# Row maxima as a stream of searches in two stages, paired float32r scores, and two score units ahead of the values

## The reference, cut to what matters

```
xn = layernorm(x)
q, k, v = split(xn @ w_qkv)          # 16 heads of 16
s = softmax(causal(q k^T / 4)) v @ w_out
f = xn
for i in range(6):
    f = gelu(f @ W1[i]^T + B1[i]) @ W2[i]^T + B2[i] + f     # 256 -> 1024 -> 256
    if i < 5: f = layernorm(f) * LN_G[i] + LN_B[i]
out = x + s * silu(f)
```

## Time and profile before

| what | us |
|---|---|
| runs of the kernel | 1800.85, 1801.35, 1807.49 (median 1801.35) |
| span of the profiled execution | 1806.1 |
| PE busy | 1716.2 |
| DVE busy | 1149.1 |
| ACT busy | 958.0 |
| POOL busy | 323.2 |

### The profile page before, as it was taken

One profiled execution on the slowest core, in us unless ns is written; L12 is line 12 of the kernel. 1 busy time (PEld: TensorE's weight loads), 2 busy tenths in 40 slices (PEclk: granted clock), 3 DMA queues, 4 the chain that ended last, 5 costly groups with the idle time before them and its releaser, 6 DMA issues. The chain is left out here.

```text
span 1806.1 us, 33624 instructions
## 1 busy us (share of the span) xinstructions
PE 1716.2 (95%) x11664; PEld 1312.9 (73%) x11664; DVE 1149.1 (64%) x2325; ACT 958.0 (53%) x1364; POOL 323.2 (18%) x317
## 2 busy tenths in 40 slices
PE   6979999999999999999999999997999989999947
PEld 5869999999999989999999998875444433444236
DVE  7846666666666656666666643366877866877326
ACT  5834555555555545555555554432666665666723
POOL 3511111111111111111111111110121211121214
PEclk9989999999999999999999999998999998999969
DMA  6940000000000000000000050003474754574113
GB/s 206 306 140 13 12 17 16 13 12 17 13 9 12 17 16 12 13 17 12 16 12 12 0 83 24 23 24 64 76 112 75 109 84 73 88 107 73 48 57 137
DMA packets 104427, 97.97 MB, mean 54 GB/s; under 512 B 26636, under 2 KB 88588, under 8 KB 104316
## 3 DMA queue, kind: packets, MB, share of 16 engines
q1 hardware_dynamic: 104256, 96.39, 23.9%
q10 hardware_dynamic: 60, 0.10, 0.0%
HBM read 62.15 MB, written 29.62 MB: 51 GB/s over the span
## 5 line engine op out<-in xcount | busy, mean ns | idle before, releaser
L626 ACT ACTIVATE m_hid<-m_h_ps,m_b1s 128x512 f32<-128x512 f32 x384 | 264.3, 688 | 571.0 <-PE m_h_ps L752 558.9
L687 DVE TENSOR_TENSOR m_hidl<-m_hid,m_hidh 128x512 fp32r<-128x512 f32 x384 | 307.4, 809 | 323.9 <-ACT m_hidh L628 322.8
L129 DVE TENSOR_REDUCE mx<-a_s_ps 128x1 f32<-128x512 f32 (+3 forms) x570 | 341.2, 656 | 91.3 <-PE a_s_ps L117 87.8
L1003 ACT ACTIVATE a_prob<-a_st_ps 128x1024 f32<-128x1024 f32 (+1 forms) x320 | 289.9, 938 | 168.5 <-PE a_st_ps L1153 123.0
L752 PE MATMUL m_h_ps<-xth,shared 128*128 (+1 forms) x768 | 269.8, 397 | 12.3 <-DVE shared L655 12.2
L763 PE MATMUL m_y_ps<-shared,m_hidh 128*128 128x256 f32 x1536 | 277.9, 281 | 0.0
L628 ACT ACTIVATE m_hidh<-m_h_ps,m_b1s 128x512 fp32r<-128x512 f32 x384 | 261.8, 682 | 0.0
L763 PEld LDWEIGHTS m_y_ps<-shared,m_hidh 128*128 128x128 f32 x1536 | 246.6, 189 | 12.0 <-DVE m_hidl L687 0.4
L602 POOL TENSOR_TENSOR y<-y,m_b2s 128x1024 f32<-128x1024 f32 x47 | 112.8, 2400 | 708.3 <-DVE y L663 708.3
L763 PE MATMUL m_y_ps<-m_w2h,m_hidh 128*128 128x256 f32 x768 | 217.9, 284 | 0.6 <-DVE m_hidl L687 0.3
L763 PE MATMUL m_y_ps<-shared,m_hidl 128*128 128x256 f32 x768 | 215.8, 281 | 0.0
(11 more groups left out here) (115 smaller groups left out, 2648.3 us busy)
## 6 DMA issues: line engine op xcount, KB each, us to landing
q_parts<-p_part SPq DMA_DIRECT2D x16, 384.0 KB, 3.5
k_parts<-p_part SPq DMA_DIRECT2D x16, 384.0 KB, 3.0
m_raw<-w1t SPq DMA_DIRECT2D x48, 128.0 KB, 2.2
m_raw<-w2t SPq DMA_DIRECT2D x48, 128.0 KB, 2.4
shared<-q_parts SPq DMA_DIRECT2D x48, 128.0 KB, 4.6
shared<-k_parts SPq DMA_DIRECT2D x48, 128.0 KB, 7.7
a_qs<-q_parts SPq DMA_DIRECT2D x48, 128.0 KB, 4.6
a_ks<-k_parts SPq DMA_DIRECT2D x48, 128.0 KB, 7.4
```

The lines of the kernel that those rows point to most:

```text
L129: return nc.vector.reduce_max(mx[:, half, first:first + heads, qt], scores, AX_X)
L626: nc.scalar.activation(hid[k % 2][:], h_ps[k % 2][:], ACT.Gelu, bias=b1s[s.par][:, k:k + 1])
L687: nc.vector.tensor_tensor(hidl[k % 4][:], hid[k % 2][:], hidh[k % 4][:].bitcast(F32), ALU.subtract).then_inc(low_done, 1)
L1003: nc.scalar.activation(prob[step % BUFS][:, j:j + heads, 0:hi - lo], unit_ps(unit), ACT.Exp).then_inc(exp_done, 1)
```

## The change

It touches nearly all of the file. In short:

* q and k are split into two float32r parts of float32 size. A stack has three parts, 48 rows a head, and two rows for the maximum. Two heads lie side by side, at partitions 0 and 64, and a product of scores is a pair of float32r matmuls, one on each half of the array's rows, into two banks. `max_pieces` gives 20 pieces a group.
* The class `MaxSearch` makes one sequence of 336 visits: for each group 20 pieces, and one turn of the maxima, placed after the fifth piece of the next group. A visit is a product on PE and a maximum on DVE. There are two PSUM banks for it, one a side. The mask at a diagonal is no product any more: DVE adds a mask tile and takes the maximum in one instruction (`tensor_tensor_reduce`). The first 209 visits are made in `mlp`, 9 in two slots, the rest in `attend`, spread over the first 14 groups. Search and scores have their own loads of the stacks; the maxima go through device memory.
* `mlp` is written out without loops. It holds the transposed rows of two groups only and turns each slot's rows in the slot before (47 turns in the loop and one ahead of it), works in `xres` in place, has one y buffer in PSUM (its sum in two halves), does one scaled pass on ACT and two on POOL, and no longer stores its rows.
* `project` loads and splits block 0's weights, and no longer stores turned rows.
* `attend` is written out, without a planner. Steps are 10 a group: the last key tile but two and the last of a half are one step of 384 + 128 columns. Each step's units are both issued, then the visits due, then the values of two steps before. `o_ps` has two buffers; DVE copies the output.
* `combine` reads the gate from `xres`.

The core of the diff:

```diff
-PARTS = 3
-STACK = 6 * HD
+PARTS = 2
+STACK = 3 * HD
 ROWS = STACK + PARTS
+SIDE = P // 2
+PAIR = 2
+N_GROUPS = BATCH * HG
+AHEAD = 10
...
+    def pe_visit(s, pe, s_ps, v):
+        m, p = s.visits[v]
+        if p == NP:
+            pe.wait_ge(s.nm_ready, m + 1)
+            pe.wait_ge(s.maxed, 2 * v)
+            s.nc.tensor.transpose(s_ps[0:PARTS * HG * QT, 0, 0:P], s.nm[:].rearrange("p a m -> p (a m)"), s.ident[:]).then_inc(s.done, 1)
+            return
...
+        for c in range(columns):
+            for side in range(2):
+                if c == 0 and v:
+                    pe.wait_ge(s.maxed, 2 * v - 1 + side)
+                rows = slice(SIDE * side, SIDE * side + STACK)
+                i = s.nc.tensor.matmul(s_ps[:, side, c * keys:(c + 1) * keys], s.q[m % 2][rows, first + c, qt * P:(qt + 1) * P],
+                                       s.k[m % 2][rows, first + c, half * BANK:half * BANK + keys], start=True, stop=True)
+        i.then_inc(s.done, 1)
...
+        if qt // HG != half:
+            s.nc.vector.reduce_max(mx[:, half, first::PAIR, qt], s_ps[:, :, 0:keys], AX_X).then_inc(s.maxed, 2)
+        else:
+            for side in range(2):
+                for c in range(columns):
+                    h = PAIR * side + first + c
+                    i = s.nc.vector.tensor_tensor_reduce(s.unused[:, v % 2, side, c * keys:(c + 1) * keys], s_ps[:, side, c * keys:(c + 1) * keys],
+                                                         s.causal[:, BANK - keys:BANK], 1.0, NEG, ALU.add, ALU.max, mx[:, half, h:h + 1, qt])
+                i.then_inc(s.maxed, 1)
...  (mlp)
+        VISITS = search.at[AHEAD, 0]
+        for v in range(VISITS):
+            slot, place = divmod(2 * v, 9)
+            AT.setdefault(CH * (1 + slot) + (1, 4, 4, 5, 5, 6, 6, 7, 7)[place], []).append(v)
...
+            for n in range(CHUNKS + 2):
+                if n < CHUNKS:
+                    up(n)
+                if n % CH == 2 and n // CH + 1 < SLOTS:
+                    turn(n // CH + 1)
+                if n >= 2:
+                    down(n - 2)
+                for v in AT.get(n, ()):
+                    search.pe_visit(pe, s_ps, v)
...  (attend)
+                if U >= 2:
+                    pe.wait_ge(exp_done, U - 1)
+                col = 0
+                for kt, lo, hi in STEPS[step][1]:
+                    for c in range(columns):
+                        for side in range(2):
+                            rows = slice(SIDE * side, SIDE * side + ROWS)
+                            to = st_ps[unit % 2][:, side, col + c * WIDTH[step]:col + c * WIDTH[step] + hi - lo]
+                            i = nc.tensor.matmul(to, ks[n % 2][rows, first + c, kt * P:(kt + 1) * P],
+                                                 qs[n % 2][rows, first + c, lo:hi], start=True, stop=True)
+                    col += hi - lo
+                i.then_inc(st_done, 1)
...
+            for at in range(ALL + LATE + 1):
+                n, step = divmod(at, NS)
+                if at < ALL:
+                    scores(n, FIRST_OF[step])
+                if at < ALL and LAST_OF[step] > FIRST_OF[step]:
+                    scores(n, LAST_OF[step])
+                for v in AT.get(at, ()):
+                    search.pe_visit(pe, s_ps, v)
+                if 0 <= at - LATE < ALL:
+                    values(at - LATE)
```

More of the change, by code:

```diff
@@ L102, in shared_stacks @@
[L102 to L118, removed]
@@ L121, in by_head @@
-def by_head(bank, piece):
-    _, _, _, heads, keys = piece
-    return bank[:, 0:heads * keys].rearrange("p (h n) -> p h n", n=keys)
-def row_max(nc, mx, scores, piece):
-    qt, half, first, heads, _ = piece
-    return nc.vector.reduce_max(mx[:, half, first:first + heads, qt], scores, AX_X)
-def project(nc, x, wqkv, scratch, keep):
+            columns = min(BANK // keys, PAIR)
+            pieces += [(qt, half, c, columns, keys) for c in range(0, PAIR, columns)]
+    return pieces
+PIECES = max_pieces()
@@ L518, in sweep @@
[L518 to L537 removed]
+        shift_ready = b.sem("m_shift_ready")
@@ new lines @@
+STEPS = attention_steps()
+NS = len(STEPS)
+WIDTH = [sum(hi - lo for _, lo, hi in parts) for _, parts in STEPS]
+UNITS = [(step, first, min(BANK // WIDTH[step], PAIR)) for step in range(NS) for first in range(0, PAIR, min(BANK // WIDTH[step], PAIR))]
+NU = len(UNITS)
+FIRST_OF = [min(n for n, unit in enumerate(UNITS) if unit[0] == step) for step in range(NS)]
+LAST_OF = [max(n for n, unit in enumerate(UNITS) if unit[0] == step) for step in range(NS)]
+LAST_STEP = [max(step for step in range(NS) if STEPS[step][0] == half) for half in range(2)]
@@ new lines, with attend @@
+DIAGONALS = [[sum(hi - lo for _, lo, hi in parts[:i]) for i, (kt, _, _) in enumerate(parts) if kt // HG == half] for half, parts in STEPS]
+SELECTS = sum(len(d) for d in DIAGONALS)
+BUFS = 3
+LATE = 2
+def attend(nc, x, wout, scratch, keep, search):
+    od = scratch["o"]
+    ALL = NS * N_GROUPS
+    VISITS = range(search.at[AHEAD, 0], len(search.visits))
+    AT = {}
+    weights = [0.5 if WIDTH[step] < BANK else 1.0 for step in range(NS)]
+    total = sum(weights) * (N_GROUPS - 2)
+    for v in VISITS:
+        due = total * (v - VISITS[0]) / len(VISITS)
+        at = 0
+        while due >= weights[at % NS]:
+            due -= weights[at % NS]
+            at += 1
+        AT.setdefault(at, []).append(v)
+    STEP_OF = {v: at for at, visits in AT.items() for v in visits}
@@ new lines, in _ @@
+            for at in range(ALL + LATE + 1):
+                for half in range(2):
+                    n, left = divmod(at - LATE - LAST_STEP[half], NS)
+                    if left == 0 and 0 <= n < N_GROUPS:
+                        copy_o(n, half)
+                for v in AT.get(at, ()):
+                    search.dve_visit(dve, s_ps, v)
+                    if v == VISITS[-2]:
+                        for step in range(3):
+                            search.dve_negate(dve, N_GROUPS - 1, step)
@@ L1190, in _, with scores @@
-            groups(pe, body)
+            def scores(n, unit):
+                step, first, columns = UNITS[unit]
+                U = NU * n + unit
+                if unit == 0:
+                    pe.wait_ge(keep["qk_loaded"][n % 2], (LOADS + NM_LOADS) * 16 * (n // 2 + 1))
+                if U >= 2:
[3 more added lines that the diff above has]
+                    for c in range(columns):
+                        for side in range(2):
+                            rows = slice(SIDE * side, SIDE * side + ROWS)
[4 more added lines that the diff above has]
+                i.then_inc(st_done, 1)
```

1312 lines of the change are left out of this document (524 added, 788 removed).

## The result

The changed kernel takes **1858.14 us** (median of 4 runs, 1855.63 to 1863.76) where the kernel before took 1802.27 beside it: ratio 1.031, interval 1.029 to 1.034. It is 3% slower. The forecast was 1752 and the range ended at 1840: sign and range were both wrong.

A forecast was written before the change was run, and what follows sets the result against it. TensorE's stream was taken to bound feed-forward and attention. Projection 106, feed-forward 1237, border 7, attention 320 and end 86.3 sum to 1756; with the profiled span 4.75 over the median, the forecast was 1752 us, range 1700 to 1840.

The forecast's parts named there:

- TensorE's stream: Feed-forward and attention: TensorE's back-to-back matmuls set the time; a feed-forward chunk is 2.80 us, a slot 23.25.
- the pairing: Search and scores: two float32r matmuls in separate row halves run side by side, one pair of 512 streaming 0.23 us.
- the visit's price: Feed-forward search: a visit costs 0.60 us for 512 keys, 0.54 for 384, mean 0.59; 122 us with the turned maxima.
- The masked form on VectorE: Search at a diagonal: a masked piece is two products of 0.69 us on VectorE, so TensorE does not wait.
- Rival 3: Masked search on VectorE takes 1.38 us for 512, so TensorE waits in feed-forward (some 58 us) and attention: 1890; chance 0.06.
- Rival 1: Halves pair but their weight loads go one after another: a visit costs 0.12 us more, 1798 in total; chance 0.13.
- They slow the splits, which have two chunks of slack: Feed-forward: POOL's two more passes a slot slow VectorE's splits, but the slack covers it; costed at nothing.
- Projection, "within -3 and +6": Projection stage: 106 us where 106.4 was, within -3 and +6, TensorE and the DMAs at alike pace.
- Attention, 320: Attention stage: groups of 19.8 us with visits and 18.6 without, 320 us against 464.8, so -145.
- if TensorE waits for VectorE's maxima: Search: a sign named in advance that would show the prediction wrong; VectorE's work was expected to lie under the pace.
- Border and end: Border to attention falls from 15.4 to 7 us; the end stays at 22.0 + 64.3, 86.3 us.
- Rival 2: Pairs in row halves do not overlap: feed-forward +43 us, attention +57, together 1852; chance 0.15.

The follow-up runs named there:

- e1: Changed kernel with the next block's last weight piece split on VectorE at chunk 4 of the slot, not chunk 7: 1831.26 us.
- e17: e8 plus paired values' loads, search loads held back to steps 5 to 8, and output stores from GpSimd at step 4, not SyncE at step 2: 1744.42 us.
- e4: Changed kernel with VectorE taking an attention step's maximum before copying an output half, not after: 1844.08 us.
- e8: Changed kernel with the edits of e1, e4 and e5 together: 1792.29 us.
- e5: Changed kernel with the projection's input rows of group g+3, not g+2, loaded at the head of round g: 1836.68 us.
- e18: Changed kernel with attention's output stores alone moved, issued from GpSimd at step 4 instead of from SyncE: 1838.37 us.
- e16: e8 with attention's four search loads held back, three of the twelve transfers at each of steps 5 to 8: 1791.29 us.
- e13: e8 with the values of two groups loaded in one transfer, rows of 512 B instead of 256 B: 1789.13 us.
- e2: Changed kernel with the next block's last weight piece split on VectorE at chunk 1 of the slot, not chunk 7: 1840.26 us.
- e6: Changed kernel with both matmuls of every search and scores pair on rows 0 to 63, so output differs: 2199.5 us.

## Why the prediction was wrong, point by point

- **TensorE's stream, the pairing, the visit's price**: right, 0.57 and 0.63 for 0.54 and 0.60. With its stops taken away (e1) the feed-forward is 1246.4 for 1237; what is left is 0.02 a chunk (2.82 for 2.80), 8 us.
- **The masked form on VectorE**: 0.685 us for 512 keys, and 0.08 for a read of its result; forecast 0.69. Rival 3 is out (its 58 us for the feed-forward don't follow from its own figures either: 12 of 20 visits in 200 pieces at 0.6 are 72). Rival 1 as well: the loads start together.
- **"They slow the splits, which have two chunks of slack"**: this step failed. True of the 384 splits of the hidden layer (0.9 us in the mean for 0.809). The forecast gave a cost in total to the weight splits and none to their place: the last one, at chunk 7 beside POOL, has no slack, and its cast grew from 0.29 to 2.5. Together 27 us, of which the place is 18.
- **Projection, "within -3 and +6"**: this step failed too. TensorE and the DMAs were taken to set the pace alike, and the order of SyncE's queue was not walked through. The load of x stands behind stores that wait: 21 us.
- **Attention, 320**: the count of engines was right, and e17 shows it: 315.8, groups of 19.2 to 19.9 where 19.8 was forecast, and ScalarE busy at 88%. The step that failed is that it had no term for transfers. The earlier trace rows has a DMA share of 0.51 over 464.8 us; the same work in 320 is 0.74 in the mean. The estimate above for the one engine could have been made from these rows and the last four stores: 0.51 of 464.8 is 237 us an engine, so 227 + 159 = 386 us of packets for it, which fit in 465 and not in 320. Of the 56 us between the changed kernel and e17 in attention, the output copy ahead of the maximum is 13 (e4). All three edits of e8 give 19; e1 and e5, which don't touch the stage, show 4 each. The other 37 are traffic: the stores, the search loads' place, the values' short rows. They act together: the stores alone gave 8 (e18), the search loads' place alone 6 (e16, 13 on top of e13), the values' rows 2 (e13), not 37.
- **The sign named in advance**, "if TensorE waits for VectorE's maxima", came true in attention (TensorE's idle time there, in the kernel after):

```profile
PE a_s_ps L164 <- DVE x_mx L180: 13.6, 13, 1.3
PE a_s_ps L164 <- DVE x_mx L185: 6.6, 12, 0.8
```

  That is 20 us. The prediction put VectorE's search and copies under ScalarE's pace by their sum, and not by their order, in which a copy stands ahead of a maximum. In e17, with the order turned, the two waits are 1.2 and 0.9 us.
- **Border and end**: 6.1 for 7; 90.0 for 86.3, and 79.2 in e17, where the stores have left SyncE, which had seemed no part of the change.
- **Rival 2's 1852** stood beside the measured 1858 with the wrong mechanism. A time that fits is no evidence; 4 ns between two starts is.

The version that the experiments point to, e17, takes 1744.42 us, 3.3% less than the kernel before and 6.1% less than the changed one. Its profiled span, 1746.8, is 9 us under the forecast's sum of 1756, but not part by part: projection 99.9 for 106, feed-forward 1248.2 for 1237, border 3.7 for 7, attention 315.8 for 320, end 79.2 for 86.3. That the sums lie close is in part luck.

## What to carry to other kernels

When a stage is to get a third shorter, divide its transfers' time by the new length before believing the engines' count; where that comes near one, the order of the queue and the shape of each transfer decide. Where one kind of transfer goes packet by packet, a new order in its queue did little: each load put first made another late (31 and 41 us worse), pacing gave 1 to 9, and moving the slow kind to GpSimd's queue gave 36. Look at the packets of a transfer that goes alone: a DMA share of 0.06 there is the sign. And an operation "with slack" has it only at the place where that was counted: look at the last one ahead of each border.

## What the hardware showed that I had not expected

- A cast of 128x256 on VectorE, 0.285 us alone, takes 2.4 to 2.5 beside a 128x1024 addition on POOL (L555 in the kernel after, the addition of B2 in e2). It ends just behind it: 759.33 and 759.19.
- Two float32r matmuls in separate row halves start 4 ns apart, and their loads 3 ns.
- In e6 the granted clock stays at 0.50 for 677 us in which TensorE is idle for 1 us in all.
- A store of 17 rows of 4 KB from SyncE's queue goes packet by packet, 2.65 us each and 10.6 for four; from GpSimd's queue the packets of four overlap and take 2.3 us. The Trainium skill (DMA: Bandwidth & Descriptors, "Issuing engines are not separate DMA queues") says that another issuing engine saves only a usually small time on the sequencer. Here e17 saved 36 us in 1780, so the measurement decides: with the issuing engine the way in which these packets were spread changed as well.
